# Four graph networks on one core: x read during the counting, the counts' finish in another order, x added to the residual earlier

## The chip, the cores and the metric

The kernel runs on one core of a Trainium2 chip. The metric is the device time of one launch in microseconds (us). The core's engines are TensorE (PE in the profile, its weight loads PEld), VectorE (DVE), ScalarE (ACT), GpSimd (POOL) and SyncE (SP); each runs its own program, and they wait for each other on semaphores.

## The reference

Input x is 1250 nodes by 768 features; 20,000 edges (`src`, `dst`) carry one of 3 types. Four blocks follow each other, each on a normalized and clipped x, and each adds to x:

```
for block in (GAT, GCN, GAT with residuals, relational GCN):
    h = relu(layernorm(x));  x = x + block(h, edges)
```

The first block normalizes h once more with a gain and a shift (`L0_norm_g`, `L0_norm_b`) before its first attention. The third block ends so, with `h1` the output of its first half:

```
h = layer_norm(attention(h1) + b2, g2, be2)
x = x + h + (h1 @ Wr2 + br2)
```

An attention is over the edges and one loop at each node: a softmax over a node's incoming edges of leaky_relu(s_src + s_dst), weighted by how often an edge occurs. The graph convolutions need, for each node and type, the number of incoming edges (degrees) and its inverse.

## The kernel before

Nodes are worked on in NT = 10 tiles of P = 125 rows. The kernel is a sequence of stages; each is a block in which every engine runs a program written out by hand, and a barrier of all engines ends it.

`count_matrices` turns the edge list into dense counts `k.counts` (node by node by type) and `k.degrees`: VectorE makes one-hot rows, TensorE multiplies them, ScalarE copies the sums out. SP loads the edges and, as groups of counts are done, writes them to DRAM (L155).

`finish_counts` then works on VectorE in this order: the degree chain (L397 to L415: the diagonal of `degrees` into `of_node`, its sum, inverses, the largest degree), the sum of the counts over types `ctot` (L416 to L422), ten `linked` tiles (which edges exist, L425), and 20 mask halves (L430), each of which waits for TensorE's transposes of `linked` into one of two PSUM banks (L450). ScalarE only takes a square root (L439); the last reciprocal (L434) waits for it, and SP writes `inv` after that (L377).

`norm_rows` normalizes ten row tiles, in a pipeline over VectorE, ScalarE and TensorE (which turns each tile). It is called five times. As "both" (tag t0, the first) it loads x itself (L858), then the two gain rows spread over all partitions (L861), which the second normalization waits for (L958). As "next" (tag t7) it closes the third block: SP loads the gains, the small tables of the next stage (`tables`), and then for each tile a residual row tile (L874) and an x tile (L876) into two slots each, and stores the new x (L868). POOL adds x to the residual (L893), VectorE adds the sum to the scaled row (L928, `shift1`), and the chain goes on with the second normalization.

`attention` (tag g3 for the third block's second attention) sums weighted rows on TensorE in 30 steps. Between them it computes `h1 @ Wr2` in 30 fill tiles (three jobs of 256 columns, ten tiles each): SP loads weights into two slots (L1783), POOL splits each into a high and a low part (L1859, L1861) in a ring of `kb + 2` = 10, TensorE multiplies (L2142), VectorE adds the bias into `fin` (L1976) and SP stores it to `res_dram` (L1789). Six fill tiles come ahead of the first step. The second normalization's shift `be2` (`more`) is added to the bias by VectorE once (L1973).

Of the kernel before, what the change touches and what calls it, by code (L numbers as in the profile page):

```python
# [15 lines left out]
F32 = mybir.dt.float32  # L16
# [52 lines left out]
class Kernel:  # L69
# [4 lines left out]
    def __init__(self, nc, ctx):  # L74
# [15 lines left out]
        self.consts = ctx.enter_context(nc.semaphore("consts"))  # L90


def count_matrices(nc, k, src, dst, etype):
# [5 lines left out]
    with ExitStack() as ctx:  # L99
# [239 lines left out]
def finish_counts(nc, k):  # L339

    with ExitStack() as ctx:
# [9 lines left out]
        of_node = sb("of_node", [P, REL, N], F32)  # L351
# [19 lines left out]
        with nc.Block(no_gpsimd_drain=True) as block:  # L371
# [15 lines left out]
            def _(dve):  # L387
                steps = [0]

                def step(ins):  # L390
# [6 lines left out]
                step(dve.tensor_tensor(of_node[:].rearrange("p r (t n) -> p (r t) n", n=P),  # L397
# [3 lines left out]
                                       of_node[:].rearrange("p r (t n) -> p (r t) n", n=P), AX, ALU.add))  # L401
# [14 lines left out]
                dve.tensor_tensor(k.ctot[:], k.counts[:, :, 0], k.counts[:, :, 1], ALU.add).then_inc(summed, 1)  # L416
                dve.wait_ge(summed, 1)
                dve.tensor_tensor(k.ctot[:], k.ctot[:], k.counts[:, :, 2], ALU.add).then_inc(summed, 1)
                dve.wait_ge(summed, 2)
                dve.tensor_tensor(diag, diag, k.ident[0:P, 0:P].unsqueeze(1).broadcast_to([P, NT - 1, P]),  # L420
                                  ALU.add).then_inc(summed, 1)
                dve.tensor_tensor(last_diag, last_diag, k.ident[0:P, 0:P], ALU.add).then_inc(summed, 1)  # L422
                dve.wait_ge(summed, 4)
                for b in range(NT):
                    dve.tensor_scalar(linked[:, b], k.ctot[:, b], 1.0, None, ALU.min).then_inc(link_ready, 1)  # L425
                for i in range(NT):
                    for h in range(2):
                        dve.wait_ge(turned, 2 * i + h + 1)

                        dve.tensor_scalar(k.mask[:, i, h * 5 * P:(h + 1) * 5 * P].rearrange("p (b s) -> p b s", s=P),  # L430
                                          ps16[0:P, h, 0:5 * PITCH].rearrange("p (b s) -> p b s", s=PITCH)[:, :, :P],
                                          -1.0, -NEG, ALU.add, ALU.mult).then_inc(mask_out, 1)
# [4 lines left out]
            def _(act):  # L437
                act.wait_ge(deg_chain, 9)
# [330 lines left out]
def norm_rows(nc, k, tag, width, rows, ht, kind, gain=None, res=None, x=None, x_out=None, ht2=None, low=None, table=None):  # L769
# [4 lines left out]
    own = rows.shape[0] != P  # L774
# [4 lines left out]
    with ExitStack() as ctx:  # L779
# [8 lines left out]
        rs = sb("rows", [P, NT, width]) if own else rows  # L788
        gb = sb("gb", [P, 2, width]) if gain else None
        add_r = sb("add_r", [P, 2, width]) if res is not None else None  # L790
        add_x = sb("add_x", [P, 2, width]) if x is not None else None
# [10 lines left out]
        r_in = [sem(f"r_in{n}") for n in range(2)]  # L802
        x_in = [sem(f"x_in{n}") for n in range(2)]
        both_in = sem("both_in")
# [47 lines left out]
        with nc.Block(no_gpsimd_drain=True) as block:  # L852
            @block.sync
            def _(sp):
# [4 lines left out]
                if gain:  # L859
# [4 lines left out]
                for i in range(NT + 2):  # L864
# [6 lines left out]
                    if i < NT and res is not None:  # L871
# [3 lines left out]
                    if i < NT and x is not None:  # L875
                        sp.dma_start(add_x[:, i % 2], x.rearrange("(t p) f -> p t f", p=P)[:, i]).then_inc(x_in[i % 2], 16)  # L876
# [6 lines left out]
            def _(pool):  # L883
# [5 lines left out]
                if kind == "next":  # L889
                    for t in range(NT):  # L890
                        pool.wait_ge(r_in[t % 2], 16 * (t // 2 + 1))
                        pool.wait_ge(x_in[t % 2], 16 * (t // 2 + 1))
                        pool.tensor_tensor(add_r[:, t % 2], add_r[:, t % 2], add_x[:, t % 2], ALU.add).then_inc(both_in, 1)  # L893

            @block.vector
            def _(dve):
                def stats1(t):
                    if own:
                        dve.wait_ge(loaded[t], 16)
                    for q in range(n_st):  # L900
# [15 lines left out]

                def scale1(t):
                    dve.wait_ge(gained, 32)
# [4 lines left out]
                def shift1(t):  # L923
                    dve.wait_ge(scaled, t + 1)
                    dve.wait_ge(inv1, t + 1)
                    if kind == "next":
                        dve.wait_ge(both_in, t + 1)
                        dve.scalar_tensor_tensor(row(t), row(t), rstd[:, 0, t:t + 1], add_r[:, t % 2], ALU.mult,  # L928
# [24 lines left out]
                def scale2(t):  # L953
                    dve.wait_ge(gained, 32)
# [667 lines left out]
def attention(nc, k, tag, heads, ch, v, parts, rows=None, given=0, bias=None, diag=None, slots=6, e=None, fill=(), more=None):  # L1622
# [59 lines left out]
    with ExitStack() as ctx:  # L1682
# [27 lines left out]
        if jobs:  # L1710
# [7 lines left out]
            fin = sb("fin", [P, 2, fw], F32)  # L1718

# [29 lines left out]
        fin_made = sem("fin_made")  # L1749
        stored = [sem(f"stored{n}") for n in range(2)]  # L1750
# [5 lines left out]
        with nc.Block(no_gpsimd_drain=True) as block:  # L1756
            @block.sync
            def _(sp):
# [26 lines left out]

                def store(f):
# [1275 lines left out]
```

## Time and profile before

| | us |
|---|---|
| median of 3 runs (4012.14 to 4022.28) | 4012.77 |
| the profiled execution | 4026.57 |
| its span | 4024.8 |
| TensorE, VectorE, ScalarE, POOL busy | 3316.1, 1775.5, 1137.4, 554.9 |

The span is what the trace covers; around it lie 1.8 us. Busy times overlap, and their shares are means over the whole span, while each stage has its own limit. A row of a timeline shows the start, the time from the first instruction of the group to the end of the last one, the engine, the line, what is written and read, and in brackets how long the engine had been idle, and what ended that.

### The profile page before, as it was taken

What the parts mean: (1) busy time and instruction counts of PE and PEld (TensorE: products, weight loads), DVE (VectorE), ACT (ScalarE), POOL (GpSimd) and SP (SyncE); (2) the same over time, 40 slices, a digit from 0 to 9 for tenths busy, and PEclk for the clock granted to TensorE, in tenths of its full rate; (3) what the DMA queues carried; (4) which work ended last, traced back from release to release, by engine and by line L of the source; (5) the groups of instructions that cost most, each with busy time, mean ns of one, the idle gap of its engine ahead of it and who ended that gap; (6) DMA issues with size and microseconds to landing.
All of it is one profiled execution on the core that took longest, in us unless ns stands there. A gap on an engine that the chain in (4) does not pass through costs nothing. (4 is left out here: it accounts for less than half of the span.)

```text
span 4024.8 us, 55608 instructions
## 1 busy us (share of the span) xinstructions
PE 3316.1 (82%) x21922; PEld 3172.7 (79%) x21923; DVE 1775.5 (44%) x3332; ACT 1137.4 (28%) x1960; POOL 554.9 (14%) x702
## 2 busy tenths in 40 slices
PE   7926578686997669993879828999999999999898
PEld 7816578575997668882868618999999999999898
DVE  6756785754232586646665451222231221311111
ACT  2304233232343422233322121222242221312212
POOL 0001000010110451112221012111111111110110
PEclk9957797687998789995989958999999999999999
DMA  1221210123112221102010122222332222311312
GB/s 23 54 61 35 44 32 8 19 75 94 30 46 74 74 37 43 49 25 87 21 39 28 43 115 70 79 73 73 93 94 60 70 75 56 86 56 44 109 53 70
DMA packets 279596, 233.25 MB, mean 58 GB/s; under 512 B 108952, under 2 KB 264513, under 8 KB 279305
## 3 DMA queue, kind: packets, MB, share of 16 engines
q1 hardware_dynamic: 166355, 163.71, 14.9%
q10 hardware_dynamic: 112950, 65.63, 5.9%
q8 instruction: 187, 3.06, 0.3%
q14 instruction: 104, 0.85, 0.1%
HBM read 195.36 MB, written 33.94 MB: 57 GB/s over the span
## 5 line engine op out<-in xcount | busy, mean ns | idle before, releaser
L2729 PE MATMUL psum<-p_w_hi,h_lo 128*125 128x384 f32 (+1 forms) x1680 | 532.5, 317 | 42.8 <-POOL p_w_lo L2498 31.6
L2730 PE MATMUL psum<-p_w_lo,h_hi 128*125 128x384 f32 (+1 forms) x1680 | 530.6, 316 | 0.0
L2732 PE MATMUL psum<-p_w_hi,h_hi 128*125 128x384 f32 (+1 forms) x1680 | 529.7, 315 | 0.0
L2790 PE MATMUL psum<-p_c_st,p_v_lo 125*128 125x312 f32 (+1 forms) x1800 | 511.8, 310 | 19.1 <-ACT p_c_st L2557 19.1
L2790 PE MATMUL psum<-p_c_st,p_v_hi 125*128 125x312 f32 (+1 forms) x1800 | 509.5, 309 | 0.0
L2123 PE MATMUL psum<-v,g_e 125*125 125x193 f32 (+4 forms) x2320 | 422.5, 341 | 104.0 <-DVE g_e L1926 103.9
L2123 PEld LDWEIGHTS psum<-v,g_e 125*125 125x125 f32 x2320 | 381.2, 200 | 136.5 <-DVE g_e L1926 61.6
L2557 ACT CAST p_c_st<-p_c 125x624 fp32r<-125x624 uint16 (+2 forms) x450 | 286.3, 679 | 400.7 <-DMA p_c<-c_dram 218.0
L2790 PEld LDWEIGHTS psum<-p_c_st,p_v_lo 125*128 125x128 f32 x1800 | 338.7, 191 | 21.1 <-ACT p_c_st L2557 21.1
L2729 PEld LDWEIGHTS psum<-p_w_hi,h_lo 128*125 128x125 f32 x1680 | 315.5, 188 | 48.4 <-POOL p_w_lo L2498 29.3
L2639 DVE TENSOR_TENSOR p_v_lo<-psum,p_v_hi 125x384 fp32r<-125x384 f32 (+1 forms) x210 | 109.1, 520 | 548.7 <-ACT p_v_hi L2573 548.7
L2790 PEld LDWEIGHTS psum<-p_c_st,p_v_hi 125*128 125x128 f32 x1800 | 338.9, 191 | 0.2
L2730 PEld LDWEIGHTS psum<-p_w_lo,h_hi 128*125 128x125 f32 x1680 | 316.0, 188 | 0.0
L2732 PEld LDWEIGHTS psum<-p_w_hi,h_hi 128*125 128x125 f32 x1680 | 315.8, 188 | 0.0
L2496 POOL CAST p_w_hi<-p_w_raw 128x384 fp32r<-128x384 f32 (+1 forms) x212 | 99.8, 471 | 1539.7 <-PE psum L2732 594.9
L2788 PE MATMUL psum<-p_v_lo,p_c_st 125*125 125x384 f32 (+1 forms) x900 | 273.3, 325 | 24.9 <-ACT p_c_st L2557 24.9
L2573 ACT CAST p_v_hi<-psum 125x384 fp32r<-125x384 f32 (+1 forms) x210 | 94.5, 450 | 660.7 <-PE psum L2732 404.8
L2788 PE MATMUL psum<-p_v_hi,p_c_st 125*125 125x384 f32 (+1 forms) x900 | 271.7, 323 | 0.0
L2695 DVE TENSOR_TENSOR p_tmp<-psum,p_scale 128x312 f32<-128x312 f32 (+1 forms) x130 | 62.8, 483 | 321.3 <-PE psum L2790 321.3
L2498 POOL TENSOR_TENSOR p_w_lo<-p_w_raw,p_w_hi 128x384 fp32r<-128x384 f32 (+1 forms) x212 | 192.9, 910 | 17.0
L2788 PEld LDWEIGHTS psum<-p_v_lo,p_c_st 125*125 125x125 f32 x900 | 168.9, 190 | 27.3 <-ACT p_c_st L2557 27.1
L2050 ACT ACTIVATE g_e<-g_e,g_cols 125x1250 f32<-125x1250 f32 x100 | 133.3, 1341 | 165.4 <-DVE g_e L1921 165.1
(266 smaller groups left out, 6185.8 us busy)
## 6 DMA issues: line engine op xcount, KB each, us to landing
p_c<-c_dram ACTq DMA_DIRECT2D x45, 761.7 KB
p_w_raw<-in_L_gnn_w_rel_dram SPq DMA_DIRECT2D x96, 192.0 KB
p_c<-c_dram ACTq DMA_DIRECT2D x30, 610.4 KB
p_c<-c_dram ACTq DMA_DIRECT2D x15, 766.6 KB
p_w_raw<-in_L_gnn_W_dram SPq DMA_DIRECT2D x84, 128.0 KB
c_dram<-counts SPq DMA_DIRECT2D x15, 610.4 KB
res_dram<-g_fin SPq DMA_DIRECT2D x70, 125.0 KB
p_scale<-inv_dram SPq DMA_DIRECT2D x54, 156.0 KB
```

The costliest lines, as they stand in the source:

```text
L2050: act.activation(e[:, m % NE], e[:, m % NE], ACT.Exp, bias=s_col[:, h, b:b + 1]).then_inc(exps, 1)
L2123: ins = pe.matmul(ps[0:P, bank, off:off + c1 - c0], w[:, t * P:(t + 1) * P], v[:, b, h, c + c0:c + c1], start=first, stop=(b == NT - 1), s ...
L2496: pool.tensor_copy(w_hi[:, slot, :w], raw).then_inc(whi_made, 1)
L2498: pool.tensor_tensor(w_lo[:, slot, :w], raw, w_hi[:, slot, :w].bitcast(F32), ALU.subtract).then_inc(w_made, 1)
L2557: act.copy(c_st[:, m % CS, :, :n], src).then_inc(c_made, 1)
L2573: act.copy(v_hi[:, t, :w], prod).then_inc(vhi_made, 1)
L2639: dve.tensor_tensor(v_lo[:, t, :w], prod, high, ALU.subtract).then_inc(vlo_made, 1)
L2729: pe.matmul(prod, lo[:, b, cols], w_hi[:, slot, :w], start=(b == 0), stop=False)
L2730: pe.matmul(prod, hi[:, b, cols], w_lo[:, slot, :w], start=False, stop=False)
L2732: ins = pe.matmul(prod, hi[:, b, cols], w_hi[:, slot, :w], start=False, stop=end)
L2788: return pe.matmul(ps[0:P, 2 + u % UB, :w], counts_at[:, off:off + size], v[:, b, :w], start=start, stop=stop, skip_group_check=True)
L2790: return pe.matmul(ps[:, 2 + u % UB, :n], v[:, b, off:off + size], counts_at[:, :n], start=start, stop=stop, skip_group_check=True)
```

## The change

Four parts.

1. In `count_matrices` SP also loads the two gain rows of the first norm and the ten tiles of x, behind the edges, into memory that is kept for the first norm (`x_rows`, `norm_gain`). The first `norm_rows` gets them (`given`, `gain_given`) and loads nothing; its first instruction on VectorE waits for all twelve loads.
2. In `finish_counts` VectorE makes `ctot` and `linked` first and the degree chain after them, in place in `k.degrees`; the 20 mask halves go to ScalarE as an activation, ahead of its square root.
3. In g3, SP loads for each fill tile its part of x (`x_bias`, three slots), and the gain rows of the last norm (`gain3`). POOL adds bias and shift once, then the bias to each x tile, behind the weight splits of the same job; VectorE's `finish` adds that tile in place of the bias. So `res_dram` holds the residual and x.
4. In the last norm ("next") the x loads, POOL's adds and the gain loads are gone; POOL issues the residual loads itself into four slots.

```
     # count_matrices, SP
+    for n, a in enumerate(gain):
+        sp.dma_start(gain_rows[:, n], a.partition_broadcast(P)).then_inc(k.x_in, 16)
+    for t in range(NT):
+        sp.dma_start(x_rows[:, t], x.rearrange("(t p) f -> p t f", p=P)[:, t]).then_inc(k.x_in, 16)
     # finish_counts: the chain of L397 to L415 moves behind L425, of_node becomes k.degrees; on ScalarE
+    for i in range(NT):
+        for h in range(2):
+            act.wait_ge(turned, 2 * i + h + 1)
+            act.activation(k.mask[:, i, h * 5 * P:(h + 1) * 5 * P].rearrange("p (b s) -> p b s", s=P),
+                           ps16[0:P, h, 0:5 * PITCH].rearrange("p (b s) -> p b s", s=PITCH)[:, :, :P],
+                           ACT.Copy, bias=NEG, scale=-NEG).then_inc(mask_out, 1)
     act.wait_ge(deg_chain, 9)
     act.activation(degree[:, REL], degree[:, REL], ACT.Sqrt).then_inc(root, 1)
     # norm_rows, "next"
-    sp.dma_start(add_x[:, i % 2], x...[:, i]).then_inc(x_in[i % 2], 16)
-    pool.wait_ge(r_in[t % 2], 16 * (t // 2 + 1))
-    pool.wait_ge(x_in[t % 2], 16 * (t // 2 + 1))
-    pool.tensor_tensor(add_r[:, t % 2], add_r[:, t % 2], add_x[:, t % 2], ALU.add).then_inc(both_in, 1)
+    if t >= RES:                                   # RES = 4
+        pool.wait_ge(y_made, t - RES + 1)
+    pool.dma_start(add_r[:, t % RES], res.rearrange("(t p) f -> p t f", p=P)[:, t]).then_inc(r_in[t % RES], 16)
     # attention g3, SP
+    def load_x(f):
+        j, t = divmod(f, NT)
+        at = sum(q.w.shape[1] for q in jobs[:j])
+        sp.dma_start(x_bias[:, f % XR, :jobs[j].w.shape[1]],          # XR = 3
+                     fill_x.rearrange("(t p) f -> p t f", p=P)[:, t, at:at + jobs[j].w.shape[1]]).then_inc(x_read[f % XR], 16)
     sp.dma_start(f_more[:], more.partition_broadcast(P)).then_inc(f_bias_in, 16)
+    for f in range(XR if jobs else 0):
+        load_x(f)
     for n in range(RAWS, kb):
         load_w(n)
+    for n, a in enumerate(ahead_in[1]):
+        sp.dma_start(ahead_in[0][:, n], a.partition_broadcast(P)).then_inc(k.gain_in, 16)
...
     store(f)
+    load_x(f + XR)
     # attention g3, POOL
+    def add_bias(f):
+        if f == 0:
+            pool.wait_ge(f_bias_in, 16 * (len(jobs) + 1))
+            pool.tensor_tensor(f_bias[:], f_bias[:], f_more[:], ALU.add).then_inc(bias_whole, 1)
+            pool.wait_ge(bias_whole, 1)
+        pool.wait_ge(x_read[f % XR], 16 * (f // XR + 1))
+        pool.tensor_tensor(x_bias[:, f % XR, :wide], x_bias[:, f % XR, :wide], f_bias[:, at:at + wide],
+                           ALU.add).then_inc(x_made, 1)
+    for j in range(len(jobs)):
+        for b in range(kb):
+            split_w(kb * j + b)
+        for t in range(NT if fill_x is not None else 0):
+            add_bias(NT * j + t)
     # attention g3, VectorE, finish(f)
-    step(dve.tensor_tensor(f_bias[:], f_bias[:], f_more[:], ALU.add))
+    dve.wait_ge(x_made, f + 1)
+    plus = x_bias[:, f % XR, :w]
-    dve.tensor_tensor(fin[:, f % 2, :w], ps[0:P, 6 + f % 2, :w], f_bias[:, at:at + w], ALU.add).then_inc(fin_made, 1)
+    dve.tensor_tensor(fin[:, f % 2, :w], ps[0:P, 6 + f % 2, :w], plus, ALU.add).then_inc(fin_made, 1)
```

## Rows read from the trace of the kernel before

**Rows 1.** The page: the span, and TensorE and VectorE over it.
```profile
span 4024.8 us, 55608 instructions
...
PE 3316.1 (82%) x21922; PEld 3172.7 (79%) x21923; DVE 1775.5 (44%) x3332; ACT 1137.4 (28%) x1960; POOL 554.9 (14%) x702
```

**Rows 2.** Busy time by stretch; columns in the first row.
```profile
core 0: us, PE busy (x) PEld busy (x) DVE busy (x) ACT busy (x) POOL busy (x), PEclk, DMA share, GB/s
...
257.20:272.30 15.10, 0.00 (x0) 0.00 (x0) 0.01 (x1) 0.00 (x0) 0.00 (x0) 0.50 0.48 34
272.30:305.70 33.40, 3.03 (x12) 2.24 (x12) 7.23 (x25) 4.21 (x8) 0.00 (x0) 0.50 0.31 123
305.70:343.40 37.70, 22.86 (x108) 19.54 (x108) 35.17 (x86) 25.77 (x62) 0.00 (x0) 0.57 0.00 1
2009.40:2062.00 52.60, 33.71 (x162) 25.99 (x162) 35.66 (x48) 14.77 (x19) 16.36 (x21) 0.74 0.20 62
2062.00:2295.50 233.50, 215.81 (x1256) 193.66 (x1256) 132.05 (x141) 60.17 (x52) 21.52 (x29) 0.96 0.08 22
2295.50:2319.40 23.90, 4.66 (x8) 0.84 (x8) 3.31 (x8) 1.87 (x3) 1.80 (x1) 0.64 0.50 156
2319.40:2402.00 82.60, 16.04 (x50) 8.14 (x50) 46.05 (x109) 18.85 (x43) 16.21 (x9) 0.52 0.31 123
2402.00:2412.00 10.00, 4.54 (x18) 3.37 (x18) 7.50 (x23) 6.39 (x13) 0.00 (x0) 0.50 0.13 38
```

**Rows 3.** The timeline of the counts' finish.
```profile
211.56 4.07 DVE L397 TENSOR_TENSOR of_node<-degrees,ident 125x3750 f32<-125x3750 f32 x1 [4.45 <-PEq L66]
...
222.58 6.67 DVE L416 TENSOR_TENSOR ctot<-counts 125x12500 uint16<-125x12500 uint16 x1
...
241.65 11.30 PE L450 MATMUL psum<-ident,linked 125*125 125x125 bf16 x80 [32.76 <-DVE linked L425]
...
255.68 0.21 DVE L434 RECIPROCAL inv<-degree 125x10 f32<-125x10 f32 x1
```

**Rows 4.** Groups on ScalarE by shape: busy us and mean ns.
```profile
L1023 ACT COPY h_t<-psum 128x500 f32<-128x500 f32 x40 | 21.6, 567 | 2.3 <-PE psum L1073 2.3
...
L1023 ACT COPY h_t<-psum 128x250 f32<-128x250 f32 x20 | 7.4, 370 | 0.0
...
L439 ACT ACT_TABLE_LOAD x1 | 1.3, 1283 | 0.8 <-PEq L66 0.8
```

**Rows 5.** The timeline of the first norm.
```profile
257.20 28.39 SPq L858 DMA_DIRECT2D t_rows<-in_x_dram  x10
...
305.68 1.02 DVE L958 SCALAR_TENSOR_TENSOR t_ring<-t_rows,t_mv,t_gb 125x768 f32<-125x768 f32 x1 [22.04 <-DMA t_gb<-in_L_gnn_norm_b_dram]
...
343.45 5.39 SPq L1232 DMA_DIRECT2D p_w_raw<-in_L_gnn_W_dram  x6
```

**Rows 6.** The last norm: its waits, VectorE's groups, and its DMA queue.
```profile
POOL t_add_r L893 <- DMA t_add_x<-x_dram: 177.7, 10, 112.4
...
DVE v L928 <- POOL t_add_r L893: 48.2, 10, 11.7
...
L920 DVE SCALAR_TENSOR_TENSOR v<-v,t_mv,t_gb 125x768 f32<-125x768 f32 x10 | 10.0, 997 | 8.8 <-DMA t_gb<-in_L_gnn_be_dram 8.8
...
q1 hardware_dynamic: 3413, 10.02, 31.1%
```

**Rows 7.** SP's writes of counts: durations, first and last start.
```profile
L155 SPq DMA_DIRECT2D c_dram<-counts x12: 750/5018/8172, 58.4 to 179.0; - x12
```

**Rows 8.** g3 and its like: an add, weight landings, POOL's operations by shape.
```profile
2037.15 0.96 DVE L1973 TENSOR_TENSOR g_f_bias<-g_f_bias,g_f_more 125x768 f32<-125x768 f32 x1 [8.25 <-PE psum L2142]
...
DMA to landing us min/median/max: 2.0/2.8/9.9
...
L2498 POOL TENSOR_TENSOR p_w_lo<-p_w_raw,p_w_hi 128x256 fp32r<-128x256 f32 x84 | 62.0, 738 | 6.7
L1342 POOL TENSOR_TENSOR v<-v,p_shift_row 125x256 f32<-125x256 f32 x40 | 48.1, 1216 | 38.7 <-DVE parts L1462 38.7
```

More of the change, by code:

```diff
@@ L394, in step @@
                     dve.wait_ge(deg_chain, steps[0])
-                step(dve.tensor_tensor(of_node[:].rearrange("p r (t n) -> p (r t) n", n=P),
+                dve.tensor_tensor(k.ctot[:], k.counts[:, :, 0], k.counts[:, :, 1], ALU.add).then_inc(summed, 1)
+                dve.wait_ge(summed, 1)
+                dve.tensor_tensor(k.ctot[:], k.ctot[:], k.counts[:, :, 2], ALU.add).then_inc(summed, 1)
+                dve.wait_ge(summed, 2)
+                dve.tensor_tensor(diag, diag, k.ident[0:P, 0:P].unsqueeze(1).broadcast_to([P, NT - 1, P]),
+                                  ALU.add).then_inc(summed, 1)
+                dve.tensor_tensor(last_diag, last_diag, k.ident[0:P, 0:P], ALU.add).then_inc(summed, 1)
+                dve.wait_ge(summed, 4)
+                for b in range(NT):
+                    dve.tensor_scalar(linked[:, b], k.ctot[:, b], 1.0, None, ALU.min).then_inc(link_ready, 1)
+                step(dve.tensor_tensor(k.degrees[:].rearrange("p r (t n) -> p (r t) n", n=P),
                                        k.degrees[:].rearrange("p r (t n) -> p (r t) n", n=P),
@@ L766, in _, with norm_rows @@
                         n += 1
-def norm_rows(nc, k, tag, width, rows, ht, kind, gain=None, res=None, x=None, x_out=None, ht2=None, low=None, table=None):
+def norm_rows(nc, k, tag, width, rows, ht, kind, gain=None, res=None, x_out=None, ht2=None, low=None, table=None, given=None,
+              gain_given=None):
     kb = width // 128
@@ L773, in norm_rows @@
     second = kind in ("both", "next")
-    own = rows.shape[0] != P
+    own = given is None and rows.shape[0] != P
     padded = not own and len(rows.shape) == 4
@@ L786, in sem @@
             return signals.new(f"{tag}_{name}")
[L788 to L791, printed above, removed]
+        rs = given if given is not None else sb("rows", [P, NT, width]) if own else rows
+        gb = gain_given if gain_given is not None else sb("gb", [P, 2, width]) if gain else None
+        RES = 4 if kind == "next" else 2
+        add_r = sb("add_r", [P, RES, width]) if res is not None else None
         ring = sb("ring", [P, R, width]) if second else None
@@ L870, in _ @@
                         tables.store(sp)
-                    if i < NT and res is not None:
+                    if i < NT and res is not None and kind == "gain":
                         if i >= 2:
@@ L899, in stats1 @@
                         dve.wait_ge(loaded[t], 16)
+                    elif given is not None and t == 0:
+                        dve.wait_ge(k.x_in, 16 * (NT + 2))
                     for q in range(n_st):
@@ L1619, in _, with attention @@
                                 spread(j, a, u)
-def attention(nc, k, tag, heads, ch, v, parts, rows=None, given=0, bias=None, diag=None, slots=6, e=None, fill=(), more=None):
+def attention(nc, k, tag, heads, ch, v, parts, rows=None, given=0, bias=None, diag=None, slots=6, e=None, fill=(), more=None,
+              fill_x=None, ahead_in=None):
     cw = min(ch, 256)
@@ L1749, in attention @@
         fin_made = sem("fin_made")
+        x_read = [sem(f"x_read{n}") for n in range(3)]
+        bias_whole = sem("bias_whole")
+        x_made = sem("x_made")
         stored = [sem(f"stored{n}") for n in range(2)]
@@ L1862, in _ @@
                                        ALU.subtract).then_inc(w_made, 1)
+                def add_bias(f):
+                    j = f // NT
+                    at = sum(q.w.shape[1] for q in jobs[:j])
+                    wide = jobs[j].w.shape[1]
+                    if f == 0:
[10 more added lines that the diff above has]
+                        add_bias(NT * j + t)
             @block.vector
```

79 lines of the change are left out of this document (41 added, 38 removed).

## The prediction

> **What bounds the kernel now.** I read the page first. TensorE is busy for 82% of a span of 4024.8 us and VectorE for 44% [rows 1]; such shares are means over stages with different limits, so I cut the span at the stages that the diff touches and read busy time by stretch [rows 2]. There the reader sees two stretches with almost no TensorE work. In the first norm stage (257.2 to 343.4) TensorE does 3.0 + 22.9 us in 86, and VectorE 0.0 + 7.2 + 35.2 = 42.4 us: until 305.7 the stage waits. In the last one (2295.5 to 2412) VectorE does 3.3 + 46.1 + 7.5 = 56.9 us in 116.5. What they wait for stands in the timeline of the first [rows 5] and in the waits of the last [rows 6]. In the first, the x loads are issued at 257.20, nothing is worked on before 272.3, and at 305.68 VectorE has waited 22.04 us for the gain rows, which queue on SP behind x. In the last, the adds of POOL wait for the x tile, and VectorE waits 48.2 us for those adds and 8.8 for the gains. The third touched stretch, the counts' finish from 211.56 to 255.9, is VectorE from end to end, in the order that its program has [rows 3]. In the fourth, the attention g3 from 2009.4 to 2295.5, TensorE is busy 33.7 and 215.8 us of 52.6 and 233.5 [rows 2], so it sets the time there, and the change should only not disturb it.
>
> **The finish of the counts.** The first degree operation starts at 211.56 and the sum of the counts at 222.58: 11.0 us that stand ahead of everything TensorE needs [rows 3]. Moved behind the ten `linked` operations, this chain runs on VectorE while TensorE transposes and ScalarE makes masks; cover is there, since masks take over 13 us. That removes 11.0 us. Three things come back. First, the masks. They now take 0.70 us a half (241.65 to 255.68, 20 halves) with VectorE [rows 3]. ScalarE's nearest rows, from PSUM, are 567 ns for 500 columns and 370 for 250, so a half of 625 should be 567 + 125 x 0.79 = 665 ns [rows 4]. With the hand-overs I take 0.75 a half, +1.0 us in all; the bounds are 0.67 (-0.6) and, if the two banks did not overlap at all, 0.70 + 0.67 = 1.37 (+13.4). I stay near the lower, because the same two banks overlap in the loop of now. Second, the square root stands behind the masks on ScalarE, and the last reciprocal, the write of inv and the stage's end stand behind it: about 0.3 us, and a table load of 1.28 if Copy and Sqrt need different sets [rows 4], together +1.6. Third, writing the product over `degrees` in place of `of_node` costs nothing, the same operation. So the finish becomes 11.0 - 1.0 - 1.6 = 8.4 us shorter (bounds 11.6 shorter, 4.0 longer).
>
> **x in the count stage.** Ten x tiles and two gain rows of 375 KB each (125 x 768 x 4 bytes) go onto SP behind the edges. At the 123 GB/s that such transfers reach [rows 2] each takes 3.1 us, 37 us for twelve. SP's next work there, the first write of counts, is at 58.4 [rows 7], and the first norm starts about 190 us later: the cover is wide, and without it only the rest would show. The edges are ahead of them in the queue, so I cost this at 0 (bounds 0 and +2, if the last edges share the engines with the first x rows). In the first norm stage nothing is then waited for except the engines. From the first x issue to the next stage's first load are 343.45 - 257.20 = 86.2 us [rows 5]. VectorE's work of 42.4 stays, and where it ran freely (305.7 to 343.4) it was idle 37.7 - 35.2 = 2.5 us [rows 2]. So 44.9 us are left, and 41.3 go. TensorE, ScalarE and the granted clock of 0.50 (1.2 GHz) don't matter there: in the free stretch ScalarE is busy 25.8 and TensorE 22.9. The write of inv, which lies ahead of x on SP today, delays nobody any more. Bounds: 43 gone (no idle time) and 38 (some idle time at the start, where each step waits for ScalarE's root).
>
> **x added in g3.** New on SP are 30 x tiles of 125 KB (1.0 us each at that rate) and two gain rows. New on POOL are 30 adds of 125x256 and one of 768 columns. From VectorE one add goes, 0.96 us, in a place where it waited 8.25 us for TensorE anyway [rows 8]. POOL's price for 256 columns is 738 ns undisturbed and 1216 beside VectorE's work [rows 8], so 22 to 36 us of its own time, with POOL busy 16.4 + 21.5 of 286 us now [rows 2]. Three x tiles are ahead of weights 2 to 7 on SP, and TensorE's first product waits for the last of these weights: +3.1. POOL is then somewhat less disturbed by VectorE, so I take +2 (bounds 0 and +5). Behind x on SP wait the stores and weight loads; loads land after 2.8 us in the median and 9.9 at most [rows 8], and a tile's x is asked for when the third tile before it is stored, in the main part some 3 x 10 us ahead (24 tiles in 233.5 us). On POOL, the weights of the next job wait behind the ten adds of this one, the last of which needs the x asked for after tile 6; the bulk of these weights can't be split before tile 9 anyway, as the ring is full. Hidden, at the cost of the first tiles.
>
> **The last norm.** Gone are 10 of its 30 row transfers, the gains and POOL's adds; the ten residual loads go to POOL's queue with four slots. The transfers now keep q1 at 31.1% of 16 engines and 123 GB/s [rows 6], which is five engines full: this stage is bound by its transfers. Two limits remain. VectorE: 56.9 us, plus 2.6 of other idle time (116.5 - 56.9 - 48.2 - 8.8), plus about 3.5 until the first residual tile is there (3.1 to move, 2.8 to land, less the work before it) gives 63.0. Transfers: 20 x 3.1 = 62 us, 4.7 for the tables (4 x 128 x 896 x 4 bytes over 16 engines at a fifth of 123 GB/s each), 2.8 for the last landing: 69.5 if POOL's loads share the same five engines, far less if not. No row shows a DMA from POOL. I take the middle, 66.2: 50.3 us gone (bounds 53.5 and 47.0, and for loads that come no faster than now see the first rival).
> The Trainium skill (DMA: Bandwidth & Descriptors, Why a DMA increments its semaphore by 16 and not by 1) says that a transfer is split over the largest number of engines up to 16 that divides its partitions, 5 for 125, which the 31.1% agrees with, and that POOL's queue spreads some copies over all 16; by that the end is VectorE's, 63.0.
>
> **Sum.** -8.4 - 41.3 + 2.0 - 50.3 = -98.0 us. The profiled execution took 4026.6 us, so it would take 3928.6. The runs' median, 4012.77, is 0.34% below it; the same 2.43% off gives **3915 us**. About 0.3% (12 us) is what a measurement of this kernel can tell from no change.
>
> **The rivals.**
> *POOL's loads come late.* POOL's operations stretch beside VectorE (738 to 1216 ns [rows 8]), and VectorE would be busy nine tenths of the last norm. If loads from POOL came only at today's pace of 9 us a tile, the 82 us of row tiles would stay, and only the start shrinks, from 23.9 us [rows 2] to some 7: 17 gone in place of 50, 3948 us. Against it: four slots give each load about 20 us. Chance 0.10.
> The Trainium skill (SBUF — State Buffer, SBUF: two separate sides) speaks against the change here: it says that a DMA issued from POOL has its descriptors written by POOL's own cores, which are locked out while certain VectorE operations hold the shared port. No run shows such a DMA yet; by that rule this rival decides.
> *g3 pays for the adds.* If TensorE waits 1.2 us in each of 30 tiles for the add, 36 us come back: 3951 (half of it, 3933). For it: VectorE's finish now waits for POOL, and its scores are queued behind it. Against: TensorE's waits there are for its own work. Chance 0.10.
> *Slower than before.* In g3 the x of a tile is asked for only after the third tile before it is stored; if landing and add take longer than that lead, every tile is late. From 3.7 us a tile on, 30 tiles eat the whole gain and 0.3% more; at 4.5 us it is 135 us, 4048. The longest landing of 9.9 plus an add of 1.2 is well under 30. Chance 0.02.
> *The finish gains nothing,* as ScalarE with a serial bank order is slower: 3923, inside the range of the forecast.
> That x wouldn't be there in time for the first norm is excluded by 37 against 250 us.
>
> **Chances and range.** The forecast's own bounds added up are -11.6 - 43 - 53.5 = -108.1, or 3905, and -8.4 - 38 + 2 + 5 - 47.0 = -86.4, or 3927 (3939 with banks that don't overlap); it has 0.75; the two rivals 0.10 each; slower 0.02; some gain lost elsewhere, but under half of it, 0.03. From 3898 to 3942 lies the forecast and most of g3's partial case, 0.8. Faster by over 0.3%: 0.96; within: 0.02; slower: 0.02.
>
> **What would show it.** The mask's operation on ScalarE, x20, near 0.67 us, and the finish some 36 us long. The first norm some 45 us with no wait for a DMA in it. In g3 fill's finish still waiting for TensorE and not for POOL. The last norm some 66 us, with VectorE's wait ahead of the add of the residual small, and for the residual's DMA. I'm wrong if that wait stays at several us a tile, or if g3 grows by more than 5 us.

## The result, and the profile after

| | before | after |
|---|---|---|
| median, us (4 runs each) | 4013.38 | 3921.46 |
| lowest to highest | 4012.14 to 4022.28 | 3920.23 to 3922.67 |
| ratio, 95% interval | | 0.9759, 0.9745 to 0.9772 |

By the medians the change takes 92 us, 2.3% of the time (2.4% by the ratio), where 98 of 4026.6 (2.43%) had been summed and 3915 us forecast. A second comparison of the same two kernels (e11) gave a ratio of 0.9756 (0.9743 to 0.9769). The profiled execution of after took 3920.23 us.

Its page: the span, and the engines' busy time, beside [rows 1].

```profile
span 3918.4 us, 55639 instructions
...
PE 3320.8 (85%) x21922; PEld 3178.5 (81%) x21923; DVE 1767.7 (45%) x3311; ACT 1149.1 (29%) x1980; POOL 567.3 (14%) x733
```

The engines' work hardly changes (VectorE loses 8 us, GpSimd and ScalarE gain 12 each); TensorE's share rises because the span shrinks. What has gone is waiting. The busy time by stretch, beside [rows 2], shows where; the stretches are the finish of the counts, the first norm, g3's first 55 us and its rest, and the last norm in three pieces.

```profile
core 0: us, PE busy (x) PEld busy (x) DVE busy (x) ACT busy (x) POOL busy (x), PEclk, DMA share, GB/s
213.20:251.00 37.80, 13.42 (x100) 11.82 (x100) 29.08 (x28) 14.24 (x22) 0.37 (x1) 0.51 0.22 50
252.30:297.00 44.70, 25.83 (x120) 21.92 (x120) 42.03 (x110) 29.95 (x70) 0.00 (x0) 0.55 0.13 1
1962.00:2016.70 54.70, 32.49 (x162) 24.64 (x162) 35.54 (x47) 13.88 (x19) 21.42 (x26) 0.81 0.30 94
2016.70:2252.90 236.20, 217.84 (x1256) 195.17 (x1256) 134.86 (x141) 60.99 (x52) 40.15 (x54) 0.95 0.12 33
2252.90:2272.90 20.00, 8.74 (x18) 1.68 (x18) 16.61 (x38) 5.93 (x13) 4.04 (x7) 0.61 0.91 229
2272.90:2305.00 32.10, 10.94 (x40) 6.58 (x40) 32.06 (x81) 14.78 (x33) 1.59 (x3) 0.59 0.40 143
2305.00:2315.00 10.00, 4.54 (x18) 3.37 (x18) 7.50 (x23) 6.38 (x13) 0.00 (x0) 0.50 0.15 47
```

The first norm has VectorE busy for 42.03 of 44.70 us: it is now VectorE's from end to end. The last norm has it busy for 16.61 + 32.06 + 7.50 = 56.17 of 62.1. In g3 GpSimd's (POOL's) busy time rises from 37.9 to 61.6 us [rows 2], and TensorE's does not change.

The timeline of the finish and of the first norm's ends, beside [rows 3, 5]:

```profile
213.21 6.67 DVE L402 TENSOR_TENSOR ctot<-counts 125x12500 uint16<-125x12500 uint16 x1 [4.47 <-PEq L66]
...
232.27 1.33 PE L455 MATMUL psum<-ident,linked 125*125 125x125 bf16 x10 [21.74 <-DVE linked L411]
...
233.94 1.34 PE L455 MATMUL psum<-ident,linked 125*125 125x125 bf16 x10 [0.34 <-ACT mask L440]
...
234.74 1.27 ACT L440 ACTIVATE mask<-psum 125x625 bf16<-125x625 bf16 x2 [0.36 <-PE psum L455]
...
235.58 1.34 PE L455 MATMUL psum<-ident,linked 125*125 125x125 bf16 x10 [0.30 <-ACT mask L440]
...
249.15 1.28 ACT L444 ACT_TABLE_LOAD   x1
250.45 0.21 ACT L444 ACTIVATE degree<-degree 125x10 f32<-125x10 f32 x1
250.76 0.21 DVE L432 RECIPROCAL inv<-degree 125x10 f32<-125x10 f32 x1 [7.66 <-ACT degree L444]
...
252.35 1.02 DVE L906 BATCH_NORM_STATS2 t_st<-x_rows 125x6 f32<-125x384 f32 x2 [1.38 <-PEq L66]
...
297.03 1.31 SPq L1243 DMA_DIRECT2D p_w_raw<-in_L_gnn_W_dram  x3
```

The sum of the counts now begins the stage. TensorE and ScalarE hand a pair of banks to and fro: ten transposes in 1.34 us, then 0.30 us in which TensorE waits for the mask, 1.64 us a pair. The table load and the square root stand behind the last mask; VectorE, done with its own work earlier, waits 7.66 us for the root, and load and root are the last 1.5 of them. VectorE takes up the first norm 1.4 us after its last reciprocal and waits for no transfer.

Groups by shape, beside [rows 4, 8], and the waits that touch the new parts, beside [rows 6]:

```profile
L440 ACT ACTIVATE mask<-psum 125x625 bf16<-125x625 bf16 x20 | 12.7, 690 | 24.0 <-PE psum L455 24.0
...
L2029 DVE TENSOR_TENSOR g_fin<-psum,g_x_bias 125x256 f32<-125x256 f32 x30 | 12.7, 423 | 84.4 <-PE psum L2195 73.2 <-POOL g_x_bias L1905 11.2
```

```profile
PE psum L2195 <- POOL g_w_lo L1893: 16.2, 11, 8.6
...
DVE g_fin L2029 <- POOL g_x_bias L1905: 11.2, 1, 11.2
...
DVE v L939 <- DMA t_add_r<-res_dram: 3.3, 2, 3.0
```

A mask half takes ScalarE 690 ns. In g3 VectorE's finish of a tile waits for GpSimd once, at the first tile, and 73.2 us for TensorE; in the last norm VectorE waits 3.3 us for the residual, where it waited 48.2 for GpSimd's adds and 8.8 for the gains [rows 6].

### The profile page after: what moved, and what is told of

It is laid out like the page before. It is cut to its first block and busy times, and to the rows that moved or that the text cites. A ratio compares the mean times of both kernels' runs of the same rounds, so it can differ in the third digit from the quotient of the medians.

```text
span 3918.4 us, 55639 instructions
## 1 busy us (share of the span) xinstructions
PE 3320.8 (85%) x21922; PEld 3178.5 (81%) x21923; DVE 1767.7 (45%) x3311; ACT 1149.1 (29%) x1980; POOL 567.3 (14%) x733
## 5 line engine op out<-in xcount | busy, mean ns | idle before, releaser
L2610 ACT CAST p_c_st<-p_c 125x624 fp32r<-125x624 uint16 (+2 forms) x450 | 286.0, 679 | 392.2 <-DMA p_c<-c_dram 209.8
```

Source lines behind the costliest of these rows:

```text
L2610: act.copy(c_st[:, m % CS, :, :n], src).then_inc(c_made, 1)
```

## The experiments

Two executions of one kernel differ by some us in places that no edit touched, so the experiments are read by stage. The table gives the length of each stage in us, by the first instruction of the next: the counting; the finish, up to the end of its last reciprocal; the first norm, up to the next stage's first load; everything up to g3; g3; the last norm; the rest.

| profile | counting | finish | first norm | to g3 | g3 | last norm | rest |
|---|---|---|---|---|---|---|---|
| before | 211.6 | 44.3 | 87.6 | 1665.9 | 286.1 | 116.5 | 1612.8 |
| e4, before again | 211.5 | 42.8 | 88.5 | 1669.5 | 286.0 | 113.9 | 1607.4 |
| after | 213.2 | 37.8 | 46.1 | 1665.0 | 290.9 | 62.1 | 1603.4 |
| e11, after again | 212.7 | 37.8 | 46.1 | 1669.1 | 286.4 | 62.0 | 1599.8 |
| e1, x read early | 213.3 | 42.8 | 46.1 | 1664.2 | 285.6 | 113.8 | 1604.9 |
| e2, the finish | 211.8 | 37.8 | 88.1 | 1669.0 | 285.9 | 114.3 | 1610.3 |
| e3, the residual | 211.6 | 42.8 | 88.1 | 1666.5 | 289.3 | 62.0 | 1607.0 |
| e5, loads on SP | 212.5 | 37.8 | 46.1 | 1669.5 | 290.0 | 71.9 | 1605.9 |
| e6, three slots | 210.6 | 43.4 | 88.1 | 1672.2 | 288.7 | 110.8 | 1603.3 |
| e7, inv later | 211.3 | 42.8 | 78.1 | 1666.5 | 288.6 | 114.1 | 1606.9 |
| e8, four banks | 213.6 | 33.5 | 46.1 | 1669.7 | 290.6 | 62.0 | 1609.4 |
| e9, weights first | 212.7 | 37.8 | 46.1 | 1662.0 | 296.2 | 61.9 | 1605.7 |
| e10, three mends | 211.5 | 33.5 | 46.1 | 1663.2 | 296.6 | 62.4 | 1602.1 |
| e12, two slots | 212.9 | 37.8 | 46.1 | 1666.4 | 289.4 | 64.3 | 1606.9 |

### The change in three pieces, and before once more

e1 is part 1 of the change alone (with the degrees' product written in place, as x lies where `of_node` was), e2 part 2, e3 parts 3 and 4.

```
 # e1: before, with
+    sp.dma_start(x_rows[:, t], x...[:, t]).then_inc(k.x_in, 16)     # in count_matrices, and the two gain rows
+    norm_rows(nc, k, "t0", ..., given=x_rows, gain_given=norm_gain)
 # e2: before, with the degree chain behind `linked` and the masks on ScalarE
 # e3: before, with
+    attention(nc, k, "g3", ..., fill_x=x_dram, ahead_in=(gain3, (w["L2_g2"], w["L2_be2"])))
+    pool.dma_start(add_r[:, t % RES], res...[:, t]).then_inc(r_in[t % RES], 16)
```

> The kernel before, with x and the first norm's gain read in the count stage as after has it; the finish keeps its order, and only its scratch tile for the degrees is dropped (the product is written in place), because x lies there now. The prediction's step: the first norm falls from 86.2 us (257.20 to 343.45) to about 45, the count stage pays 1 to 2 us for the shared transfers (after's trace has 1.65), so 4013 - 41.3 + 1.65 = about 3973 us, and the finish keeps its 44 to 46 us. Rival A: half of the gain came from the finish's new order (the write of the inverse degrees leaves earlier, VectorE is free earlier): then this part alone gives less, the norm takes 50 us or more, 3980 or above. Rival B: the transfers of x steal more from the count stage when nothing else is changed: the finish would begin 5 us or more later.

> The kernel before with the finish's reorder alone: the degree chain behind the links, the masks on ScalarE. The prediction's sum for this step is -8.4 us, 4013 to 4005; after's trace reads -6.6 (44.3 us to 37.8), 4006.5, because a pair of mask and transposes cycles in 1.64 us there where two VectorE evictions took 1.40. Rival: nothing is gained in the time, since the first norm then only waits longer for x (its first wait grows from 22.0 us by as much as the finish shrank): 4013. In before x's loads are issued behind the inverse degrees' write, which itself ends with the finish, so I expect the first norm to move up whole: its VectorE start to SP's next stage stays at 86 us.

> The kernel before with x added into the residual's tiles in the last attention, the last norm's gain read there, and the residual's loads issued by GpSimd over four slots; count stage, finish and first norm as before. The prediction's sum is -50.3 for the last norm and +2 for the attention, 4013 to 3965; after's trace reads 62.7 us for the last norm (-53.8) and +4.1 for the attention, 3963. Rival A, the attention pays more for the adds alone than the whole kernel's trace shows (stores leave later, +10 or more): 3970 or above. Rival B, part of the missing 4 us between the stages' sum (about -96) and the measured -92 lies here: 3967.

> The kernel before, unchanged, profiled once more: its first profile ran 4026.57 us against a median of 4013, so 13 us of that trace are no property of the kernel. Theory: the excess is spread over the stages in which TensorE sets the time (from about 345 to 2295 us, and behind 2412 us), with a granted clock nearer to 0.90 than to 0.891, and the two norms and the finish read the same to 1 us (86.2, 116.5 and 44.3). Rival: the excess lies in one of the norms, and the change's gain there is then smaller than the two traces say.

On this chip before has a median of 4024.2 us. e1 has a ratio of 0.9903 (0.9887 to 0.9918), 39 us; e2 0.9979 (0.9969 to 0.9990), 8 us; e3 0.9881 (0.9862 to 0.9899), 48 us. Together 95 us, against 97 for the whole change by its ratio: the parts add up, and none needs another. In e1 the first norm falls to 46.1 us with the old finish ahead of it, so rival A falls, and the counting grows by 1.8 us, not by 5, so rival B does too. In e2 the first norm keeps its 88.1 us, so it moved up whole, as expected.

e4's single execution took 4021.4 us, near this chip's median, with a span 5.2 us below that of the first profile. The rest is 5.4 us shorter, but, against what was expected, so are the last norm by 2.6 and the finish by 1.5, and the stretch up to g3 is longer by 3.6. So part of the gain that the first two traces show in the touched stages (4 us, less the 0.9 by which e4's first norm is longer) is the first profile's own. Stretches that no edit touched cover 1662 to 1672 us and 1600 to 1613 us over the fourteen profiles.

### Why the finish gained less: two banks and the clock

The finish is 42.8 us in e1, e3, e4 and e7, not the 44.3 from which the sum was made. The masks of e4, in VectorE's timeline, and the busy time by stretch around them:

```profile
243.82 1.02 DVE L430 TENSOR_SCALAR mask<-psum 125x625 bf16<-125x625 bf16 x2 [0.42 <-PE psum L450]
245.26 0.88 DVE L430 TENSOR_SCALAR mask<-psum 125x625 bf16<-125x625 bf16 x2 [0.42 <-PE psum L450]
...
253.26 0.88 DVE L430 TENSOR_SCALAR mask<-psum 125x625 bf16<-125x625 bf16 x2 [0.26 <-PE psum L450]
```

```profile
241.00:245.30 4.30, 3.47 (x28) 3.16 (x29) 2.48 (x7) 0.00 (x0) 0.00 (x0) 0.51 0.00 0
245.30:248.00 2.70, 2.01 (x25) 1.60 (x23) 2.17 (x6) 0.00 (x0) 0.00 (x0) 1.00 0.00 0
```

At 245 us the granted clock goes from 0.50 to 1.00 (1.2 to 2.4 GHz), and a pair falls from 1.44 to 1.14 us. In the first profile that came at 252 us. In after it does not come at all: 0.51 over the whole finish. The other profiles agree: in all six with VectorE's masks the clock rises inside the loop, in all six with ScalarE's over two banks it does not. e8 tests whether the two banks are the reason.

```
-    if n >= 2:
-        pe.wait_ge(mask_out, n - 1)
+    if n >= 4:
+        pe.wait_ge(mask_out, n - 3)
-    ins = pe.transpose(ps16[0:P, h, ...
+    ins = pe.transpose(ps16[0:P, n % 4, ...      # and the mask reads bank (2 * i + h) % 4
```

> The kernel after with one difference: the masks' transposes go round four banks of PSUM in place of two. After's finish has a cycle of 1.64 us a pair, 1.34 of ten transposes and 0.30 of TensorE waiting for ScalarE's mask; in the kernel before, with VectorE's shorter evictions, the cycle began at 1.44 and fell to 1.14 us when the granted clock rose from 0.50 to 1.00 in the middle of the loop, at 245 us in three traces and at 252 in one. Theory 1: the wait for a bank holds TensorE back, and its gaps hold the clock down; with four banks the transposes run on, the clock rises in the loop, and ScalarE's own 0.65 us a half sets the pace: ten pairs in about 13 us in place of 16.4, the finish 34.4 us in place of 37.75, some 3 us of 3921. Theory 2: ScalarE is the pace now, and banks change nothing: 37.7 us.

The timeline of e8's masks, and its busy time by stretch:

```profile
232.71 10.90 PE L455 MATMUL psum<-ident,linked 125*125 125x125 bf16 x100 [21.74 <-DVE linked L411]
...
233.54 11.79 ACT L440 ACTIVATE mask<-psum 125x625 bf16<-125x625 bf16 x20 [20.75 <-PE psum L455]
245.34 1.28 ACT L444 ACT_TABLE_LOAD   x1
```

```profile
235.00:240.00 5.00, 4.77 (x51) 4.47 (x50) 4.96 (x2) 5.00 (x10) 0.00 (x0) 0.70 0.18 40
240.00:245.00 5.00, 2.93 (x32) 2.18 (x30) 2.64 (x12) 5.00 (x10) 0.37 (x1) 0.98 0.01 3
```

The transposes run as one group in which no wait for a mask shows, the clock rises inside the loop, and ScalarE is busy without a gap: 20 halves in 11.8 us, 0.59 each. The finish takes 33.5 us, 4.2 less, more than expected; theory 1 holds for the stage, except that the clock has no part in the gain. Busy time by stretch of e8's masks, up to the clock's rise and behind it:

```profile
233.54:238.10 4.56, 4.56 (x46) 4.56 (x45) 4.53 (x2) 4.56 (x8) 0.00 (x0) 0.51 0.32 71
238.10:245.33 7.23, 4.60 (x52) 3.55 (x50) 4.54 (x12) 7.23 (x13) 0.37 (x1) 0.97 0.01 2
```

ScalarE is busy all the time at 0.51 as at 0.97, so with four banks it sets the pace at either clock: what e8 took away is the wait for a bank. Why the clock rose with VectorE's masks over two banks and not with ScalarE's is not settled; the rows show that ahead of the rise in e4 TensorE was busy 3.47 us of the 3.76 since its first transpose, without a wait for a mask, and that in after it waited 0.30 us in each pair. The first profile of before shows no such wait either, and there the rise came only 11 us behind the first transpose. In the whole time e8 can't be told apart from after: ratio 0.9753 (0.9736 to 0.9770).
The Trainium skill (TensorE: Matmul & The Clock Gate, A second HAM failure mode: psum-queue depth-cycling) tells of a kernel that cycles through PSUM banks and in which TensorE idles so often between groups of matmuls that the clock swings between its two levels. The traces agree in part: the short idle times are there, but the clock of after does not swing, it stays at 0.50 through the loop; with four banks it is 0.98 in the loop's second half.

### Where the last norm's time went: transfers, and which queue

e6 keeps before's plan and only adds room: three slots each for the residual and x, so that three pairs of loads are issued at once. Against its expectation they stand behind the gains and the tables, as before's first two pairs do. e5 keeps after's plan, and SP issues the residual loads, four of them ahead of the tables.

```
 # e6: before, with
-    add_r = sb("add_r", [P, 2, width]);  add_x = sb("add_x", [P, 2, width])
+    RES = 3;  add_r = sb("add_r", [P, RES, width]);  add_x = sb("add_x", [P, RES, width])
+    for t in range(RES): load_both(t)                 # behind gains and tables; later pairs behind a store
 # e5: after, with
-    pool.dma_start(add_r[:, t % RES], res...[:, t]).then_inc(r_in[t % RES], 16)
+    sp.dma_start(add_r[:, t % RES], res...[:, t]).then_inc(r_in[t % RES], 16)      # four ahead, then behind each store
```

> The kernel before with three slots in place of two for the residual and for x in the last norm, the first three pairs of loads issued ahead of the gains and tables, later pairs behind the store that frees their slot; x is still read there and GpSimd still adds it. It tells apart why the stage took 114 to 116 us. Theory 1, the prediction's: its 30 row transfers of 3.0 to 3.1 us keep the queue's few engines full; then slots change little, the ten tiles keep some 9 us each, and the stage stays above 105. Theory 2: the two slots and the round trip (store behind the norm, load behind the store, add behind the load) set the 9 us a tile, and the engines are full only by the way; then three slots and the early start bring it to 80 to 95 us, 20 to 35 us faster, and much of the change's gain there could have been had without touching the attention.

> The kernel after with one difference: the ten residual loads of the last norm are issued by SP (the first four ahead of the tables, then one behind each row's store) and not by GpSimd. The prediction's bounds for this stage were 69.5 us if loads and stores share the same few engines and 63.0 if VectorE sets the end; after's trace has 62.1. Theory 1: it is the queue that made the difference; then SP's loads and stores share it, and the stage grows to about 69 us, the time by 7 us. Theory 2: loads do not bind in either queue once x is out of them; the stage stays within 2 us of 62. Theory 3, the rule against loads from GpSimd: they are slowed beside VectorE; then SP's loads come sooner and the 3.3 us that VectorE waits for the residual in after shrink, the stage falls to about 59.

SP's first loads in e6's last norm, and busy time by stretch:

```profile
2302.85 0.27 SPq L862 DMA_DIRECT2D t_gb<-in_L_gnn_g_dram  x1
...
2309.17 0.37 SPq L866 DMA_DIRECT2D t_add_r<-res_dram  x1
```

```profile
2302.80:2322.80 20.00, 5.11 (x8) 0.86 (x8) 3.31 (x8) 1.87 (x3) 0.00 (x0) 0.59 0.53 162
2322.80:2403.00 80.20, 16.68 (x50) 8.61 (x50) 45.38 (x108) 18.84 (x43) 18.00 (x10) 0.52 0.32 128
```

More slots gave 3 us of 114: e6's ratio is 0.9990 (0.9977 to 1.0003), and the share of the DMA engines stays at 0.32 with 128 GB/s for 80 us, as in before [rows 2]. The transfers were the bound and not the slots, theory 1; the earlier start that the expectation counts with was not made, as the first row load is issued 6.3 us into the stage. Busy time by stretch of e5's last norm:

```profile
2255.80:2275.80 20.00, 1.16 (x2) 0.25 (x3) 12.52 (x29) 2.45 (x5) 0.00 (x0) 0.50 0.57 160
2275.80:2317.70 41.90, 16.74 (x58) 8.20 (x57) 38.94 (x96) 19.63 (x44) 0.00 (x0) 0.62 0.33 129
```

With x gone but all rows on SP, the same 0.33 and 129 GB/s stand behind the first 20 us, and the stage takes 71.9 us, 10 more than after; the ratio is 0.9779 (0.9757 to 0.9801). In the first 20 us after shows 0.91 and 229 GB/s, e5 0.57 and 160. So taking x, its adds and the gains out is worth 114 - 72 = 42 us, and moving the loads from SP to GpSimd the other 10, near the number of e5's theory 1. Where the 10 lie, the waits say, two rows of e5 and then one of after:

```profile
PE psum L2929 <- DMA et_raw<-in_L_gnn_w_root_dram: 23.9, 1, 23.9
DVE et_both L2942 <- ACT et_high L2936: 6.6, 2, 5.9
```

```profile
PE psum L2929 <- DMA et_raw<-in_L_gnn_w_root_dram: 12.3, 1, 12.3
```

In e5 the tables stand behind four residual tiles on SP, and VectorE waits 6.6 us for their product, which it does not do in after; for the residual itself it waits 3.7 us, hardly longer than 3.3. From VectorE's last operation to the next stage e5 takes 3.6 us, after 1.0. So e5 changes two things, the queue and the tables' place in it, and no run takes them apart. That GpSimd's loads use engines which SP's rows leave idle shows in after behind the tables, with row tiles alone in flight; the first row is the last residual load, the others are busy time by stretch:

```profile
2284.81 0.53 POOL L895 DMA_DIRECT2D t_add_r<-res_dram  x1 [5.71 <-DVE v L939]
```

```profile
2286.00:2288.00 2.00, 0.38 (x2) 0.41 (x3) 2.00 (x5) 1.66 (x4) 0.00 (x0) 0.50 0.73 261
2290.00:2292.00 2.00, 0.00 (x0) 0.00 (x0) 2.00 (x7) 0.18 (x2) 0.00 (x0) 0.50 0.32 131
```

The Trainium skill (DMA: Bandwidth & Descriptors, Why a DMA increments its semaphore by 16 and not by 1) has the rule by which SP's queue spreads 125 rows over 5 of the 16 engines, and says that GpSimd's can use all for some copies. The traces agree: 0.32 and 0.33 with SP's rows alone, 0.73 with a load of GpSimd's beside them.
The Trainium skill (SBUF — State Buffer, SBUF: two separate sides) warns that loads issued from GpSimd stall beside certain VectorE operations. Here VectorE was busy 56.2 of 62.1 us and waited 3.3 us for those loads, so that stall did not decide.

e12 halves the slots of after.

```
-    RES = 4 if kind == "next" else 2
+    RES = 2
```

> The kernel after with two slots in place of four for the residual tiles of the last norm, loads still from GpSimd. Theory 1, the prediction's answer to its first rival: four slots are what keeps late loads away; a load lands in 5.6 to 10.2 us and is asked for behind the norm of the second tile before it, some 5 us, so VectorE waits 1 to 4 us a tile and the stage grows from 62 to 75 us or more. Theory 2: the loads have slack even so, since the second statistics and transposes lie between; the stage stays within 4 us of 62.

VectorE's wait for the residual in e12:

```profile
DVE v L939 <- DMA t_add_r<-res_dram: 5.4, 3, 2.8
```

The stage takes 64.3 us, in a single execution, and VectorE waits 5.4 us for the residual in place of 3.3: theory 2. Four slots are worth 2 us.

### How much of the first norm was the write ahead of x

e7 is before, with the write of the inverse degrees behind the loads of x and the gains.

```
-    sp.dma_start(k.inv_dram..., k.inv[:], allow_slow_non_contiguous=True).then_inc(k.inv_out, 16)    # finish_counts
+    sp.dma_start(k.inv_dram..., k.inv[:], allow_slow_non_contiguous=True).then_inc(k.inv_out, 16)    # t0, behind the gains
```

> The kernel before with the write of the inverse degrees issued behind the loads of x and the gains, not ahead of them. It tells how much of the 42 us that the early read of x took from the first norm is the transfer of x, and how much the write that lay ahead of it on SP (the first x row is worked on 15.1 us after its issue, and in that stretch only 34 GB/s are moved). Theory 1: the write held x back; x is there 12 to 13 us sooner, the stage from the finish's end to the next stage's first load falls from 88 to about 75 us, 4013 to 4000. Theory 2: the write shares the engines with x wherever it stands, or its slow elements come due later in the stage; then the stage stays at 85 to 88.

VectorE's waits in e7's first norm, and then in e4's:

```profile
DVE t_ring L958 <- DMA t_gb<-in_L_gnn_norm_b_dram: 22.1, 1, 22.1
DVE t_st L901 <- DMA t_rows<-in_x_dram: 11.0, 4, 7.0
```

```profile
DVE t_ring L958 <- DMA t_gb<-in_L_gnn_norm_b_dram: 22.0, 1, 22.0
DVE t_st L901 <- DMA t_rows<-in_x_dram: 21.5, 4, 17.4
```

The wait for the first rows of x falls by 10.5 us and the stage from 88.5 to 78.1; the ratio is 0.9968 (0.9952 to 0.9983). So a quarter of the 42 us was one small write (19.5 KB) with a slow pattern ahead of x in the queue, and moving it by itself was worth 10 us. The wait for the gains, behind x, did not move: that part needs x read early.

### What g3 pays, and two mends

e9 puts g3's weights ahead of bias rows and x on SP; e10 adds e8's banks and holds the loads of x in the counting until the edges are there; e11 is after, unchanged, on the same chip.

```
 # e9: after, with
+    for n in range(RAWS, kb): load_w(n)          # now ahead of f_bias, f_more and the first x tiles
 # e10: e9 and e8, with
+    sp.wait_ge(edges_in, 48)                     # ahead of the loads of the gains and x
```

> The kernel after with one difference: in the attention g3, SP issues the first job's weights 2 to 7 ahead of the bias rows and the three x tiles. In after the first of these weights is there 17.2 us after the stage's start (13.3 in before), TensorE's longest wait for a split weight is 8.6 us (3.8), and the stage takes 290.9 us (286.1). Theory 1, the prediction's step: the x tiles ahead of the weights are what the stage pays; it falls to 286 or below (the bias rows are out of the way too), 5 us of 3921. Theory 2: VectorE's finish of a tile, which waits for GpSimd's add (11.2 us once), is the price; then the stage stays near 291 or grows, because x now comes later. The start may also be bound by the scores' chain, in which case earlier weights give nothing: 290 as well.

> The kernel after with three mends: the weights ahead of x in g3, four PSUM banks for the masks (alone they brought the finish from 37.75 to 33.5 us), and the loads of x in the count stage held until the edges are there (the stage's end came 1.65 to 1.75 us later in every kernel that reads x there). Sum of the stages: -4.2, -1.7 and 0 to -5, so 6 to 11 us below after on the same chip. Rival: the finish of the counts is shorter, and what it saves is lost in the stages behind it, whose length differs by 5 us from one profile to the next anyway; the times can't be told apart.

> The kernel after, unchanged, beside the two mended ones on the same chip: ratio to before 0.976 as in the first comparison, stages as in its first trace (finish 37.8, first norm 46.1, g3 290.9, last norm 62.1) to 1 us.

Ratios: e9 0.9776 (0.9762 to 0.9789), e10 0.9761 (0.9747 to 0.9774), e11 0.9756 (0.9743 to 0.9769). The mends gained nothing, and e9's theory 1 falls: g3 grew to 296 us. The timeline of e9's g3 shows the new wait:

```profile
1988.49 1.80 POOL L1902 TENSOR_TENSOR g_f_bias<-g_f_bias,g_f_more 125x768 f32<-125x768 f32 x1 [7.40 <-DMA g_f_more<-in_L_gnn_be_dram]
...
1991.19 0.42 DVE L2029 TENSOR_TENSOR g_fin<-psum,g_x_bias 125x256 f32<-125x256 f32 x1 [12.30 <-POOL g_x_bias L1905]
...
1991.53 1.29 DVE L2011 TENSOR_TENSOR g_l_lo<-h_t,g_l_hi 128x1000 fp32r<-128x1000 f32 x1
...
1992.97 0.55 PE L2195 MATMUL psum<-g_w_hi,g_l_lo 128*125 128x256 f32 x1 [7.29 <-DVE g_l_lo L2011]
```

The third weight is there 6.2 us after the stage's start (17.2 in after), but the bias row now is the late one. GpSimd waits 7.40 us for it, VectorE's finish of the first tile 12.30 for GpSimd, and behind that finish, in VectorE's order, stands the operand that TensorE then waits 7.29 us for. Theory 2 named the wait, but not its cause, which is the bias row and not x. An order with the bias rows first, the weights next and x last was not tried.

e11 also corrects a reading. Its g3 took 286.4 us, where the first profile of after had 290.9. Over six profiles with g3 as in before the mean is 286.8 (285.6 to 288.7), over six as in after 289.4 (286.4 to 290.9): the change costs g3 some 2.6 us, about as much as one execution differs from the next.

In e10 the finish and the counting keep what they gained (33.5 and 211.5 us), and the next stage's first load is issued 5.4 us earlier than in e11; g3 loses it again.

## Why the prediction was right, step by step

The sum was -8.4 - 41.3 + 2.0 - 50.3 = -98.0 us; e4's and e11's stages, with the mean for g3, give -5.0 + 1.2 - 42.4 + 2.6 - 51.9 = -95.5. That the totals lie so close is in part luck: the finish gave 3.4 us less than predicted and the counting took 1.2, while the two norms gave 1.1 and 1.6 more.

*The finish, -8.4, measured -5.0 against e4 (-6.6 against the profile of the sum).* Moving the chain and the late square root with its table load came as worked out. Mis-sized were the masks: +1.0 us was taken, at 0.75 a half against 0.70 [rows 3]. Counted in the same way, from the first transpose to the last mask, a half costs 0.84 in after (232.27 to 249.15 us), +2.8 in all, and 11.0 - 2.8 - 1.6 are the 6.6. The step read the old finish as VectorE's from end to end, and the 0.70 as a pace at which the banks overlap. But in that loop VectorE waited 4.2 us for TensorE, with evictions of 488 ns:

```profile
L430 DVE TENSOR_SCALAR mask<-psum 125x625 bf16<-125x625 bf16 x20 | 9.6, 488 | 4.5 <-PE psum L450 4.2
```

What set the pace over two banks, as e8 shows for ScalarE, was the way round one bank: transposes, hand-over, eviction, and transposes again. ScalarE's 690 ns were foreseen as 665; that the 0.20 us by which they exceed VectorE's would come whole on each pair (1.44 to 1.64 us at the same granted clock) was not. The other 1.6 us against e4 are before's own, whose clock rose at 245 us there and at 252 in the first profile.

*x in the count stage, 0 with a bound of +2.* The counting ends at 213.0 us in the mean of the seven profiles that read x there without holding it, and at 211.4 in the six of the old order: 1.6 us, near the upper bound. With the loads held until the edges are there (e10) it ends at 211.5.

*The first norm, 44.9 us.* Measured 44.7 from VectorE's first instruction to the next stage's first load, VectorE busy for 42.03 of it against the 42.4 read from before [rows 2]. This step, 41 of the 98 us, was right in mechanism and size, because the free stretch of before already showed the pace.

*g3, +2.* Measured about +2.6. The named way, the weights behind x, is in the rows (TensorE's longest wait for one 8.6 us; it was 3.8 in before), but that it is the price is not shown: e11 has 7.0 us of that wait in a g3 of 286.4, and e9, which shortens it to 2.9, brought another wait.

*The last norm, 66.2 us between 63.0 and 69.5.* Measured 62.1, 0.9 below the end set by VectorE. The other end, 69.5 with shared engines, is e5's case, at 71.9. Both limits were the right ones; the middle was the wrong choice, since GpSimd's queue does bring other engines into use.

Of the rivals, GpSimd's late loads did not come, but the reason given against them (four slots) was not what kept them away, as e12's one execution shows. That g3 pays for the adds would have been 18 to 36 us; VectorE's finish waited for an add once in 30 tiles.

## What to carry to other kernels

Look for stretches in which no engine works, and ask which transfer is late and what lies ahead of it in its queue; then move the read into an earlier stage with idle queues, and price what remains by a stretch of the same trace where the engines already run free. Before moving a transfer, read the share of the DMA engines: a queue that holds a third of them full is a bound that more slots did not lift here, while fewer bytes and a second queue did. In a loop over few buffers, price the whole way round one buffer and not the eviction alone. A mend at the head of a queue delays what it passes: name who waits for that, in the engine's own order, before counting its gain.

## What the runs showed of the hardware

- A loop of ten transposes and two evictions over two PSUM banks stayed at a granted clock of 0.50 (1.2 GHz) when TensorE waited 0.30 us in each 1.64 (after), and rose to 1.00 (2.4 GHz) in the loop's middle at 1.44 us a pair (245 us in e4, 252 in the first profile). Over four banks, with TensorE busy without a gap, it rose 5 us behind the first transpose (e8).
- At the same granted clock of 0.50 a pair over two banks took 1.44 us with evictions of 488 ns (before) and 1.64 with 690 ns (after).
- One queue of SP moved row tiles of 125 x 768 at 123 to 129 GB/s with 0.31 to 0.33 of the DMA engines, with two, three and four slots (before, e6, e5). The last norm's first 20 us, tables among their transfers, moved 160 GB/s at 0.57 with all loads on SP (e5) and 229 at 0.91 with the residual's on GpSimd's queue (after).
- A write of 19.5 KB with a slow pattern, ahead of x on SP, held x back by 10 us (e7).
